# A Mamba-style mixer with a mixture of experts: the float32r operands are given other byte addresses in SBUF

## The reference

```python
# block 1, per batch of 1024 tokens
x = conv3(x @ w1.T); x = silu(x)
delta = softplus(x @ dl_w.T + dl_b)                 # 512 wide
A_cum = cumprod(exp(-delta * (x @ A_w.T + A_b)), axis=1)
h = cumsum((x @ B_w.T + B_b) * A_cum, axis=1)
s = h @ C_w.T + C_b + x @ D_w.T + D_b
out = s + (s * silu(s @ w2.T)) @ w3.T
# block 2, over all 4096 tokens: 8 experts, the best 2 of each token, and a shared expert
probs = softmax(xn @ router_w); top 2, renormalised
out = sum_e comb[:, e] * (silu(clip(gate_e)) * up_e) @ down_w[e]  +  shared expert
```

## Time and profile before

| what | value |
|---|---|
| median of 3 runs | 1201.09 us (1200.34 to 1205.66) |
| span of the profiled execution, first to last instruction | 1198.4 us |
| TensorE busy | 1107.5 us (92%), 7492 matmuls |
| VectorE, ScalarE, GpSimd busy | 834.3, 657.5, 305.2 us |
| experts, first gate_up to last down | 469.7 to about 1152.5 us |
| behind the last matmul | about 46 us |

### The profile page before, as it was taken

How to read it: one execution, slowest core, us unless ns; L and a number is a source line. 1 busy time by engine, 2 the same in 40 slices (tenths; PEclk the granted TensorE clock), 3 DMA queues, 4 the chain that set the end, 5 groups by cost and what they waited for, 6 DMA issues and landing times.

```text
span 1198.4 us, 23315 instructions
## 1 busy us (share of the span) xinstructions
PE 1107.5 (92%) x7492; PEld 983.6 (82%) x7492; DVE 834.3 (70%) x2113; ACT 657.5 (55%) x1325; POOL 305.2 (25%) x358
## 2 busy tenths in 40 slices
PE   3989999899979999999999999999999999999940
PEld 2665776677657566999999999999999999999940
DVE  5986898797888676566666666666666666666645
ACT  6768866768674364444444444444444444444425
POOL 1142132623441633121122122112212211221224
PEclk9999999999999999999999999999999999999985
DMA  8655765964665789432231155465912356211239
GB/s 301 220 191 178 256 212 181 322 228 153 212 228 173 261 278 345 133 71 53 53 70 31 22 161 180 167 197 176 359 22 35 95 198 215 35 32 21 35 90 207
DMA packets 96617, 191.70 MB, mean 160 GB/s; under 512 B 8768, under 2 KB 59456, under 8 KB 96576
## 3 DMA queue, kind: packets, MB, share of 16 engines
q1 hardware_dynamic: 80160, 170.38, 41.3%
q0 software_dynamic: 16416, 20.85, 10.1%
HBM read 295.62 MB, written 86.41 MB: 319 GB/s over the span
## 4 chain that ended last, share of the span: by engine, by line
PE 78%; DVE 8%; issue 4%; DMA 3%; POOL 3%; ACT 2%; SPq 1%; another core or an unknown queue 0%; DVEq 0%; ACTq 0%; POOLq 0%
PE bank L1332 12%; PE bank L1333 12%; PE bank L1334 12%; PE bank L459 11%; PE bank L1345 6%; PE bank L1343 6%; PE bank L1344 6%; PE bank L453 4%; PE bank L454 4%; PE bank L455 4%; POOL xs_scratch L1139 2%; PE bank L1320 1%; DVE a_cum L864 1%; DVE xr L1473 1%; DVE h L891 1%
## 5 line engine op out<-in xcount | busy, mean ns | idle before, releaser
L1282 POOL DMA_INDIRECT acc_scratch<-cv,ids x78 | 129.4, 1659 | 558.7 <-DVE cv L1421 517.7
L1442 DVE TENSOR_SCALAR cv<-bank 128x256 f32<-128x256 f32 x312 | 132.3, 424 | 200.2 <-PE bank L1334 197.7
L1332 PE MATMUL bank<-h_hi,w_both 128*128 128x256 f32 x936 | 269.9, 288 | 0.2 <-DVE cv L1449 0.2
L1333 PE MATMUL bank<-h_hi,w_both 128*128 128x256 f32 x936 | 262.9, 281 | 0.0
L1392 ACT ACTIVATE cv<-cv 128x256 f32<-128x256 f32 x312 | 131.0, 420 | 240.0 <-DVE cv L1442 239.1
L1334 PE MATMUL bank<-h_hi,w_both 128*128 128x256 f32 x936 | 262.2, 280 | 0.0
L1384 ACT ACTIVATE h_hi<-cv 128x256 fp32r<-128x256 f32 x312 | 130.4, 418 | 114.9 <-DVE cv L1449 114.4
L1332 PEld LDWEIGHTS bank<-h_hi,w_both 128*128 128x128 f32 x936 | 176.5, 189 | 0.4 <-issue 0.4
L1334 PEld LDWEIGHTS bank<-h_hi,w_both 128*128 128x128 f32 x936 | 176.8, 189 | 0.0
L1333 PEld LDWEIGHTS bank<-h_hi,w_both 128*128 128x128 f32 x936 | 176.5, 189 | 0.0
L1449 DVE TENSOR_TENSOR cv<-bank,cv 128x256 f32<-128x256 f32 x312 | 132.5, 425 | 48.0 <-ACT cv L1392 47.9
(11 more groups left out here) (227 smaller groups left out, 2395.2 us busy)
## 6 DMA issues: line engine op xcount, KB each, us to landing
w_both<-w_split SPq DMA_DIRECT2D x228, 768.0 KB
xs_hi<-w_split SPq DMA_DIRECT2D x38, 768.0 KB
xs_lo<-w_split SPq DMA_DIRECT2D x38, 768.0 KB
e_raw<-w_e SPq DMA_DIRECT2D x64, 384.0 KB
w_split<-e_high SPq DMA_DIRECT2D x64, 384.0 KB
w_split<-e_raw SPq DMA_DIRECT2D x64, 384.0 KB
u<-xs_scratch SPq DMA_DIRECT2D x40, 260.0 KB
x_in<-x SPq DMA_DIRECT2D x8, 512.0 KB
```

Of the source, the lines that this page charges most:

```text
L1332: nc.tensor.matmul(out, e_hi[f][:, cols], xg_hi[:, par, c, :], start=c == 0, stop=False)
L1333: nc.tensor.matmul(out, e_hi[f][:, cols], xg_lo[:, par, c, :], start=False, stop=False)
L1442: nc.vector.tensor_scalar(gate[:, f % 4, :], gu_ps[f % 2][:, 0:G], CLIP, -CLIP, ALU.min, ALU.max).then_inc(clipped, 1)
```

## The change

The tensors are declared in another order. `w_both`, `w_full` and `ones` move from `program` into `mixer`; nothing else is added or removed, and every instruction, wait and size stays.

```diff
-        w_hi, w_lo = w_both[:, 0:W_COLS], w_both[:, W_COLS:2 * W_COLS]
+        w_full = sb("w_full", [P, F_COLS])
+        ones = sb("ones", [P, HALF])
         x_in = sb("x_in", [P, LT, D])
         u = sb("u", [P, DC, L + 2])
         cv = sb("cv", [P, DC, L])
-        xs_hi, xs_lo, delta, decay, a_cum, bx, h, carry_a, carry_h, h_hi, h_lo, s, g, xr
         xnt = sb("xnt", [P, XS, DC, HALF])
+        n2 = sb("n2", [P, 2, HT, ROW])
         w_sh = sb("w_sh", [P, S_COLS])
-        n2 = sb("n2", [P, 2, HT, ROW])
+        e_raw = sb("e_raw", [P, WS, CW])
...
         slot_now = sb("slot_now", [P, 2, HT, K], I32)
-        e_raw = sb("e_raw", [P, WS, CW])
+        w_both = sb("w_both", [P, 2 * W_COLS], F32R)
+        xs_hi = sb("xs_hi", [P, DC, L], F32R)
+        xs_lo = sb("xs_lo", [P, DC, L], F32R)
+        h_hi = [sb(f"h_hi{i}", [P, HC, HALF], F32R) for i in range(2)]
+        h_lo = [sb(f"h_lo{i}", [P, HC, HALF], F32R) for i in range(2)]
+        delta, decay, a_cum, bx, h, carry_a, carry_h, s, g, xr
         e_high = sb("e_high", [P, WS, CW])
```

More of the change, by code:

```diff
@@ L57, with mixer @@
 XS = 5
-def mixer(nc, x, w_e, w_s, weights, full, consts, shared, xs_dram, x1_dram, acc_dram, fill, w_both, w_full, vec, ident,
-          tok_id, pad, zeros, ones, neg_half, tables, group_expert, group_change, group_row, group_code, out):
+def mixer(nc, x, w_e, w_s, weights, full, consts, shared, xs_dram, x1_dram, acc_dram, fill, vec, ident,
+          tok_id, pad, zeros, neg_half, tables, group_expert, group_change, group_row, group_code, out):
     with ExitStack() as ctx:
@@ L122, in mixer @@
         slot_now = sb("slot_now", [P, 2, HT, K], I32)
-        e_raw = sb("e_raw", [P, WS, CW])
+        w_both = sb("w_both", [P, 2 * W_COLS], F32R)
[3 more added lines that the diff above has]
+        h_lo = [sb(f"h_lo{i}", [P, HC, HALF], F32R) for i in range(2)]
+        delta = sb("delta", [P, 2, HALF])
+        decay = sb("decay", [P, 2, HALF])
+        a_cum = sb("a_cum", [P, HALF])
+        bx = sb("bx", [P, HALF])
+        h = sb("h", [P, 2, HALF])
+        carry_a = sb("carry_a", [P, HC])
+        carry_h = sb("carry_h", [P, HC])
+        s = sb("s", [P, DC, HALF])
+        g = sb("g", [P, DC, HALF])
+        xr = sb("xr", [P, HT, D])
         e_high = sb("e_high", [P, WS, CW])
+        w_hi, w_lo = w_both[:, 0:W_COLS], w_both[:, W_COLS:2 * W_COLS]
         start_row, limits, group_no, number = tables
@@ L1528, in program @@
         neg_half = sb("neg_half", [P, LT])
[L1529 to L1542, removed]
+        mixer(nc, d["x"], d["w_e"], w_s,
+              [(DL_AT, d["dl_w_t"], DC), (A_AT, d["A_w_t"], DC), (B_AT, d["B_w_t"], DC), (C_AT, d["C_w_t"], HC),
+               (DD_AT, d["D_w_t"], DC)],
+              [(W1_AT, d["w1_t"], DC), (W2_AT, d["w2_t"], DC), (W3_AT, d["w3_t"], DC), (RT_AT, d["router"], DC)],
+              d["vecs"], [(SGU_AT, d["sgu"], DC), (SDN_AT, d["sdn"], SC)], xs_dram, x1_dram, acc_dram,
+              fill, vec, ident, tok_id, pad, zeros, neg_half, tables,
+              group_expert, group_change, group_row, group_code, out)
 def kernel(**inputs):
```

## The result

The changed kernel takes 1208.35 us (median of 14 runs, 1202.92 to 1212.65), the kernel before in the same runs 1200.55 us. The ratio is **1.0052**, 95% interval 1.0033 to 1.0070: slower by about 6 us (4 to 8 by the interval; the two medians stand 7.8 us apart), where 30 us less was forecast.

The account below looks back on a forecast made before the run. TensorE was taken as the bound, alone in the experts' chain. Experts 26 us and mixer 4 us less bring 1198.4 to 1168 us; with the median 2.7 us above the span, 1171 us, range 1162 to 1187.

Parts of the forecast that it names:

- TensorE alone bounds the experts, and every nanosecond of a step counts: Experts: from 520 to 1140 us the chain of waits consists of TensorE alone, so each matmul's length counts.
- The fast steps therefore follow the buffer and not the slot in the order: Experts: chunk 7 takes 113.6 ns a step by its buffer at 102048, others about 118.2.
- No float32r operand lies under 102048: Experts: with all operands high, steps fall from 118.3 to 113.6 ns, 26 us less over 39 groups.
- Mixer, 4.6 to 9.1 ns a product: Mixer: 864 products of 512 columns each get that much faster, 4 us less in time, bounds 0 to 7.9.
- Does TensorE stay the bound, do reloads matter, do the lowered tensors cost: Experts keep TensorE as bound, reloads cause no counted wait, and tensors moved lower cost 0 us.
- The lengths of 595, 396 and 397 ns: Plain float32 products (595) and mixer products with h_lo (396) and h_hi (397), cited as showing no effect of place.
- Rival A: Experts: the pair's address doesn't matter, chunk 7 is fast for another reason; 1201 us, chance 0.07.
- Rival B: Experts: operands at 157952 or above cost like low ones; 1204 us, chance 0.09; partial case about 1183 us, chance 0.08.
- Rival C: All 5616 expert products: places above 157952 clash more; 125 ns a step would give 1239 us, chance 0.04.
- The rule of the Trainium skill: TensorE: independent read ports and no waiting, no address named; the change would be worth 0, time 1201 us.

Follow-up runs that it names:

- Experiment 7: Expert-order matmuls on zeros at the addresses of the kernel before, also with the buffers of chunks 6 and 7 exchanged: groups of 17.46 and 17.47 us.
- The map: Matmuls of a gate_up alone on zeros, no other engine at work, for 151 pairs of stationary and moving addresses: 113.3 to 120.2 ns a step.
- experiment 6: Kernel after with h_hi and h_lo as one tensor and shifted expert reads: ratio 0.9886, again 0.9883; then only the mixer's distance changed to 160: 0.9902.
- experiment 1: The map: gate_up matmuls alone on zeros over 151 address pairs; 502 or 512 matmuls in 60 us throughout the sweeps over regions.
- experiments 3 and 2: Kernel after with ten small tensors ahead of w_both: 1200.41 us; with six ahead of h_hi0 and four ahead of h_hi1 instead: 1182.19 us.

## Why the prediction was wrong

- *TensorE alone bounds the experts, and every nanosecond of a step counts*: right. All kernels above moved with their steps.
- *"The fast steps therefore follow the buffer and not the slot in the order"*: this is the step that failed. Gate_up and down of chunk 7 do stand in different slots, and chunk 4's down in one of these slots was slow. But slot and buffer were never exchanged in the trace: chunk 7 always came behind the same products. Experiment 7 exchanged them, and the fast steps stayed.
- *"No float32r operand lies under 102048", so all take 113.6 ns*: the 26 us rested on it. The map shows no effect of the place from 20480 to 192512. The table of first bytes in this document, read modulo 256, holds the cause: 160 and 64 before, 0 after. I compared high with low and never the low bits with each other. The term was 26 us less and came out as 9.2 us more.
- *Mixer, 4.6 to 9.1 ns a product*: the size came out (5 ns), for another reason, distance 0 in place of 96 and 160. In place of the 4 us of time, 5.0 us are seen in one pair of profiles at equal clock and 3.2 us in the fit of experiment 6; the medians of that experiment don't show it for certain.
- *Does TensorE stay the bound, do reloads matter, do the lowered tensors cost*: nothing of it came up. From 550 to 1100 us there is no wait of TensorE in any of these kernels; between 480 us and the last group there is only one, for the second group's token rows, of 0.5 us before and 0.7 us after. The lengths of 595, 396 and 397 ns that the prediction leaned on are modelled and say little; from start to start the wide plain products take 429 ns before and after.
- *Rival A* (the address of the pair doesn't matter) leaves room for chunk 7's place in the order as the cause of its fast steps, and that half is right; but addresses do matter. *Rival B* (the fast place ends above) would have read the slow steps as a border between 143071 and 157952; experiment 1 has no such border. *Rival C* came nearest in sign, with a wrong mechanism and size: it has the mean step rise above 119.4, and it rose to 120.0. B and C argued over places, and no rival named the low bits.
- *The rule of the Trainium skill*, page "SBUF — State Buffer", section "Who interferes with whom", that "PE and ACT never wait on anyone": as far as other engines go the runs agree, since groups without any other engine last as long as in the kernel, to 0.04 us. The same page of the Trainium skill has the two read ports of TensorE as independent; the steps speak against independence in cost, since the price of a product depends on the distance between what the two read, by 6.7 ns of 120, but no run shows that the ports are where it arises. By the rule the time would have been 1201 us, nearer than the forecast.
- The evenness of a mean hid the clue. The steps of one gate_up in `w_both` ran between 116 and 123 ns, in the same order two groups later, which a fixed cost of a place would not do.

## What to carry to other kernels

For float32r products with a new stationary operand each time, look at the byte addresses of the stationary and the moving operand modulo 256, and measure the distances that the kernel can have in its own order of products; here moving two buffers by 192 and 320 bytes was worth 18 us (1200.41 against 1182.19 us, experiments 3 and 2 on one chip), and a view that starts some columns further on gives each stage its own distance. Tensors declared one behind the other with sizes that are multiples of 256 bytes fall on distance 0, one of the two cheapest for 512 columns and the dearest for 256 in the order of this kernel. Before two kernels are compared by one profile each, compare their granted clocks: here the mixer's clock differed by 0.02 between the two profiles of experiment 6. And a natural experiment inside one trace separates two causes only if each occurs without the other.

## What the runs showed of the hardware

- The step of a float32r product of 256 columns lies between 113.3 and 120.2 ns at clock 1.00 in the map, mostly by the distance of its operands' addresses modulo 256; for 512 columns between 226.6 and 234.7. At distance 0, moving both by a multiple of 32 bytes changes nothing (by 16 or 48 bytes it gives 118.3), nor does moving either by a multiple of 8192. A move of the stationary operand by 256 changed the step at two of seven distances.
- One pair of distances can hold two prices (113.5 and 118.3 ns over eleven steps of chunks 7 and 6 in experiment 7), depending on the products before; the pattern repeats, with groups of 17.46 and 17.47 us in turn.
- Plain float32 products of 512 columns start 429 ns apart before and after (median), though their operands moved.
- A kernel of matmuls alone reproduced the group of the whole kernel to 0.04 us, so such a stage can be tuned on its own.
- What inside TensorE or SBUF makes this is not shown, nor are distances that are no multiple of 32 in a whole kernel.
